# Experts' results of the last layer: weighted on leaving PSUM and added in DRAM, instead of read back and weighted at the end

## The reference, cut to what matters

```
logits = xn @ w_gate                       # xn = layernorm(h), 8 experts
top_p, top_i = top_k(softmax(logits), 2)
top_p = top_p / sum(top_p)                 # = 1/(1+e) and e/(1+e), e = exp(l2 - l1)
y_e(x) = gelu(x @ w_up[e]) @ w_down[e]     # 192 -> 768 -> 192
out = h + top_p[0] * y_i0(xn) + top_p[1] * y_i1(xn)
```

## Time and profile before

| | us |
|---|---|
| median of 3 runs (612.25 to 617.3) | 615.44 |
| profiled execution, own time | 616.41 |
| its span | 614.6 |
| PE / DVE / ACT / POOL busy | 492.7 / 325.0 / 205.1 / 143.8 |
| last mixture of experts: first gather to last result | 414.51 to 593.57 |
| from there to the end of the span | 21.0 |

### The profile page before, as it was taken

The page is one execution under the profiler, slowest core; times in us unless marked ns, Lnnn a source line. Parts: engine busy times, 40 slices in busy tenths (PEclk is TensorE's granted clock), DMA queues, the critical chain, the costliest instruction groups (busy, mean ns, idle before and its releaser), DMA issues.

```text
span 614.6 us, 12430 instructions
## 1 busy us (share of the span) xinstructions
PE 492.7 (80%) x4338; PEld 453.3 (74%) x4339; DVE 325.0 (53%) x1046; ACT 205.1 (33%) x438; POOL 143.8 (23%) x148
## 2 busy tenths in 40 slices
PE   4999999887523493699999599627999999999960
PEld 4999996466522393589999586616999999999950
DVE  1578999688999886122221576782222222222207
ACT  3620024666993164044333142150321112121110
POOL 1591000000001001334421100005345444443220
PEclk9999999899557785799999799757999999999995
DMA  8991000000004003956669300027866655667126
GB/s 311 409 335 34 1 1 1 1 3 1 0 1 181 2 2 138 241 168 180 177 202 366 127 2 0 1 103 211 237 194 194 204 171 161 185 178 204 42 63 270
DMA packets 35379, 81.41 MB, mean 132 GB/s; under 512 B 7142, under 2 KB 18242, under 8 KB 34306
## 3 DMA queue, kind: packets, MB, share of 16 engines
q1 hardware_dynamic: 29762, 69.37, 34.3%
q0 software_dynamic: 5568, 11.41, 6.5%
HBM read 70.33 MB, written 10.42 MB: 131 GB/s over the span
## 4 chain that ended last, share of the span: by engine, by line
PE 69%; DVE 17%; ACT 5%; DMA 3%; issue 3%; SPq 1%; another core or an unknown queue 1%; ACTq 0%; POOL 0%; DVEq 0%; POOLq 0%
PE ps L1102 18%; PE ps L858 14%; PE ps L1078 12%; PE ps L1086 6%; PE ps L798 2%; DVE h L1878 2%; PE ps L970 1%; PE ps L838 1%; PE ps L839 1%; PE ps L942 1%; DVE xT L1722 1%; PE ps L1069 1%; PE ps L823 1%; PE ps L943 1%; DVE arena L1586 1%
## 5 line engine op out<-in xcount | busy, mean ns | idle before, releaser
L1102 PE MATMUL ps<-arena,xn 128*128 x696 | 123.2, 328 | 3.9 <-ACT xn L748 3.1
L1102 PEld LDWEIGHTS ps<-arena,xn 128*128 128x128 f32 x696 | 111.8, 190 | 6.2 <-issue 6.0
L491 POOL DMA_INDIRECT xT<-rows,from_i x58 | 56.2, 969 | 180.5 <-DVE from_i L1736 121.8
L1078 PE MATMUL ps<-xn,arena 128*128 128x128 f32 x696 | 91.0, 282 | 5.2 <-DMA arena<-ffn_b 3.2
L858 PE MATMUL ps<-arena 128*128 128x192 f32 (+1 forms) x588 | 86.3, 339 | 8.7 <-ACT arena L530 8.7
L1078 PEld LDWEIGHTS ps<-xn,arena 128*128 128x128 f32 x696 | 87.7, 198 | 6.9 <-DMA arena<-ffn_b 5.6
L858 PEld LDWEIGHTS ps<-arena 128*128 128x128 f32 (+1 forms) x588 | 84.8, 199 | 8.9 <-ACT arena L530 8.3
L1761 DVE COPY xn<-ps 128x128 f32<-128x128 f32 x58 | 16.9, 292 | 126.7 <-PE ps L1070 94.9
L504 POOL DMA_INDIRECT made<-xT,to_i x58 | 57.2, 985 | 109.8 <-DVE xT L1773 66.6
L751 ACT ACTIVATE xn<-ps 128x384 f32<-128x384 f32 x78 | 32.6, 493 | 126.5 <-PE ps L1088 99.7
L748 ACT ACTIVATE xn<-ps,b_all 128x128 f32<-128x128 f32 x114 | 30.9, 390 | 46.8 <-PE ps L1088 35.3
(11 more groups left out here) (367 smaller groups left out, 773.9 us busy)
## 6 DMA issues: line engine op xcount, KB each, us to landing
arena<-ffn_a SPq DMA_DIRECT2D x58, 384.0 KB
arena<-ffn_b SPq DMA_DIRECT2D x116, 96.0 KB
arena<-x_blocks SPq DMA_DIRECT2D x16, 384.0 KB, 7.1
arena<-x_strips SPq DMA_DIRECT2D x3, 1536.0 KB, 11.9
arena<-ffn SPq DMA_DIRECT2D x4, 1152.0 KB
rows<-xn SPq DMA_DIRECT2D x8, 384.0 KB, 2.3
arena<-made SPq DMA_DIRECT2D x4, 768.0 KB, 6.6
arena<-tok_w SPq DMA_DIRECT2D x8, 288.0 KB, 7.3
```

The lines of the kernel that those rows point to most:

```text
L491: pool.indirect_dma_start(sx[:, k % 6], None, F["src"], bass.IndirectOffsetOnAxis(from_i[:, k:k + 1], 0)).then_inc(sem(f"sx_in{k % 6}"), 16)
L1078: pe.matmul(ps[:, up_bank(u, c // 3), 128 * (c % 3):128 * (c % 3) + 128], w_up[:, u, 128 * c:128 * c + 128], sT[:, u, 0:128], start=(c % 3 ...
L1102: mm = pe.matmul(ps[:, result_bank(k, N), 0:DIM], hT[:, u % 2, 128 * c:128 * c + 128], F["w2"][:, bass.ds(e2 + DIM * c, DIM)], start=(c == ...
```

## The change

The first expert stage and all matmuls stay. In the last stage:

- Routing makes the two weights early (DVE, before the scan): e goes into column 193 of a 200-wide row of `xw`, 1/(1+e) into column 192. ACT writes the norm into columns 0 to 191, and SP writes these rows of 800 bytes to DRAM, now after `probs` as well. The gather fetches them.
- `to_i` is the token's row. `to_use` holds, for each slot, whether its token uses it as second expert. When a tile is turned, two more DVE instructions of one column each make `p_slot`: 1/(1+e) and a factor that is 1 or e. The gather of tile k + 10 waits for `p_slot` instead of the turning.
- `result` multiplies by both numbers as it takes the result out of PSUM.
- `made1` holds one row a token. SP writes `h` into it in one DMA once `h` is final (`h_row` 14), and, near the program's start, finite numbers into the rows of the empty slots. The scatter adds to its rows (`compute_op` add), and POOL issues each only when the one before has landed.
- At the end SP copies these rows to `out` in one DMA from DRAM to DRAM. Reading back, adding on DVE and the four writes are gone.

```diff
+ROW = 200
...
-                  seg=C_SEG + E0 * 16, src=rows1, made=made1)
+                  seg=C_SEG + E0 * 16, made=made1)
...
-        pk = sb("pk", [128, 2, NTOK])
...
-        sx = xT0[:, 0:6 * DIM].rearrange("p (a b) -> p a b", a=6)
-        yo = xT0[:, 6 * DIM:9 * DIM].rearrange("p (a b) -> p a b", a=3)
-        got = [xn[:], view(0, [2 * NTOK, DIM])]
+        sx = xT0[:, 0:6 * ROW].rearrange("p (a b) -> p a b", a=6)
+        yo = xT0[:, 6 * ROW:6 * ROW + 3 * DIM].rearrange("p (a b) -> p a b", a=3)
+        xw = view(E1 * HCH * DIM, [NTOK, ROW])
+        wide_rows = made0.rearrange("r c -> (r c)")[0:TOKS * ROW].rearrange("(r c) -> r c", c=ROW)
+        to_use = sb("to_use", [128, 2, 40])
+        p_slot = sb("p_slot", [128, 2, 6])
...
+            sp.wait_ge(sem("cst_in"), 16)
+            sp.dma_start(made1[TOKS + 1:TOKS + 1 + 128 * TILES1, :].rearrange("(k p) c -> p k c", p=128),
+                         cst[:, C_ID:C_ID + DIM].unsqueeze(1).to_broadcast([128, TILES1, DIM])).then_inc(sem("sums_set"), 16)
+
             def rows_out(F):
 
+                if F["n"]:
+                    sp.wait_ge(sem("probs"), 1)
                 for i in range(4):
                     sp.wait_ge(sem("xn_act"), 4 * (1 + F["n"]) + i + 1)
-                    sp.dma_start(F["src"].rearrange("(b t) c -> b t c", t=NTOK)[:, 4 * i:4 * i + 4, :],
-                                 xn[:, 4 * i:4 * i + 4, :]).then_inc(sem(f"rows_out{F['n']}"), 16)
+                    dst, src = ((rows0, xn), (wide_rows, xw))[F["n"]]
+                    sp.dma_start(dst.rearrange("(b t) c -> b t c", t=NTOK)[:, 4 * i:4 * i + 4, :],
+                                 src[:, 4 * i:4 * i + 4, :]).then_inc(sem(f"rows_out{F['n']}"), 16)
...
-            def outputs_in(F):
-
-                n = F["n"]
+            def results_landed(F):
+
                 for u in range(3):
-                    sp.wait_ge(sem(f"y_st{n}{u}"), 16 * ((F["tiles"] + 2 - u) // 3))
-                made = F["made"][0:F["sel"] * TOKS, :].rearrange("(b r) c -> b r c", b=IMGS)
-                for i in range(4):
-                    r = slice(4 * F["sel"] * i, 4 * F["sel"] * (i + 1))
-                    sp.dma_start(got[n][:, r, :], made[:, r, :]).then_inc(sem(f"back_{i}"), 16)
+                    sp.wait_ge(sem(f"y_st{F['n']}{u}"), 16 * ((F["tiles"] + 2 - u) // 3))
...
-            outputs_in(F0)
+            results_landed(F0)
+            for i in range(4):
+                sp.dma_start(xn[:, 4 * i:4 * i + 4, :], made0[0:TOKS, :].rearrange("(b t) c -> b t c", t=NTOK)[:, 4 * i:4 * i + 4, :]
+                             ).then_inc(sem(f"back_{i}"), 16)
+            sums = made1[0:TOKS, :].rearrange("(b t) c -> b t c", t=NTOK)
+            sp.wait_ge(sem("h_row"), 14)
+            sp.dma_start(sums, h[:]).then_inc(sem("sums_set"), 16)
             rows_out(F1)
             up_weights(F1)
-            outputs_in(F1)
-            for i in range(4):
-                sp.wait_ge(sem("h_final"), i + 1)
-                sp.dma_start(out[:, 4 * i:4 * i + 4, :], h[:, 4 * i:4 * i + 4, :]).then_inc(sem("out_done"), 16)
-            sp.wait_ge(sem("out_done"), 64)
+            results_landed(F1)
+            sp.dma_start(out, sums).then_inc(sem("out_done"), 16)
+            sp.wait_ge(sem("out_done"), 16)
...
+                rows, width, turned = (rows0, DIM, "x_ps0") if n == 0 else (wide_rows, ROW, "p_slot")
+
                 def load(k):
-                    pool.indirect_dma_start(sx[:, k % 6], None, F["src"],
+                    pool.indirect_dma_start(sx[:, k % 6, 0:width], None, rows,
                                             bass.IndirectOffsetOnAxis(from_i[:, k:k + 1], 0)).then_inc(sem(f"sx_in{k % 6}"), 16)
 
...
-                        pool.wait_ge(sem(f"x_ps{n}"), k - 5)
+                        pool.wait_ge(sem(turned), k - 5)
...
                 for k in range(N):
                     pool.wait_ge(sem(f"y_out{n}"), k + 1)
+                    if n and k == 0:
+                        pool.wait_ge(sem("sums_set"), 32)
+                    if n and k:
+                        pool.wait_ge(sem(f"y_st1{(k - 1) % 3}"), 16 * ((k - 1) // 3 + 1))
                     pool.indirect_dma_start(F["made"], bass.IndirectOffsetOnAxis(to_i[:, k:k + 1], 0), yo[:, k % 3],
-                                            None).then_inc(sem(f"y_st{n}{k % 3}"), 16)
+                                            None, compute_op=(ALU.bypass, ALU.add)[n]).then_inc(sem(f"y_st{n}{k % 3}"), 16)
                     if k + 10 < N:
-                        pool.wait_ge(sem(f"x_ps{n}"), k + 5)
+                        pool.wait_ge(sem(turned), k + 5)
                         load(k + 10)
...
-                        ins = act.activation(xn[:, t, :], h[:, t, :], ACT.Identity, bias=stat[:, 480 + t:481 + t], scale=stat[:, 464 + t:465 + t])
+                        ins = act.activation((xn[:], xw)[n][:, t, 0:DIM], h[:, t, :], ACT.Identity, bias=stat[:, 480 + t:481 + t], scale=stat[:, 464 + t:465 + t])
...
-            act.activation(d16, d16, ACT.Exp).then_inc(sem("soft_exp"), 1)
+            act.activation(xw[:, :, DIM + 1], d16, ACT.Exp).then_inc(sem("soft_exp"), 1)
...
                 if n:
                     dve.tensor_tensor(d16, c16, a16, ALU.subtract).then_inc(sem("soft_in"), 1)
+                    dve.memset(xw[:, :, DIM + 2:ROW], 0.0)
+                    dve.wait_ge(sem("soft_exp"), 1)
+                    link(dve.tensor_scalar(c16, xw[:, :, DIM + 1], 1.0, None, ALU.add))
+                    dve.reciprocal(xw[:, :, DIM], c16).then_inc(sem("probs"), 1)
...
-                dve.scalar_tensor_tensor(to_i[:, 0:N], row, 0.5 * n, none, ALU.add, ALU.add).then_inc(sem("places"), 1)
-                if n:
-                    dve.wait_ge(sem("soft_exp"), 1)
-                    link(dve.tensor_scalar(c16, d16, 1.0, None, ALU.add))
-                    link(dve.reciprocal(pk[:, 0, :], c16))
-                    dve.tensor_tensor(pk[:, 1, :], d16, pk[:, 0, :], ALU.mult)
+                if n == 0:
+                    dve.tensor_tensor(to_i[:, 0:N], row, none, ALU.add).then_inc(sem("places"), 1)
+                else:
+                    dve.wait_ge(sem("places"), 3)
+                    token, second = rt[:, 1280:1280 + N], to_use[:, 1, 0:N]
+                    link(dve.tensor_copy(token, from_i[:, 0:N]))
+                    dve.tensor_tensor(to_i[:, 0:N], token, none, ALU.add).then_inc(sem("places"), 1)
+                    link(dve.scalar_tensor_tensor(second, token, -2.0, row, ALU.mult, ALU.add))
+                    link(dve.tensor_scalar(second, second, 0.5, ROUND, ALU.add, ALU.add))
+                    dve.tensor_scalar(to_use[:, 0, 0:N], second, -1.0, ROUND + 1, ALU.mult, ALU.add)
+                    link(dve.tensor_scalar(second, second, ROUND, None, ALU.subtract))
...
                     dve.tensor_copy(sT[64:128, u, 128:256], ps[0:64, 0, 128:256]).then_inc(sem(f"x_out{n}"), 1)
+                    if n:
+                        dve.tensor_copy(p_slot[:, 0, u:u + 1], sx[:, u, DIM:DIM + 1])
+                        dve.scalar_tensor_tensor(p_slot[:, 1, u:u + 1], sx[:, u, DIM + 1:DIM + 2], to_use[:, 1, bass.ds(k, 1)],
+                                                 to_use[:, 0, bass.ds(k, 1)], ALU.mult, ALU.add).then_inc(sem("p_slot"), 1)
...
                     dve.wait_ge(sem(f"b_ps{n}"), k + 1)
+                    if n:
+                        dve.wait_ge(sem("p_slot"), k + 1)
                     at_least(dve, sem(f"y_st{n}{u % 3}"), 32 * j + 16 * (u // 3))
                     if n == 0:
                         ins = dve.tensor_tensor(yo[:, u % 3], ps[:, result_bank(k, N), 0:DIM], b2_all[:, bass.ds(e, DIM)], ALU.add)
                     else:
-                        ins = dve.tensor_copy(yo[:, u % 3], ps[:, result_bank(k, N), 0:DIM])
+                        ins = dve.tensor_scalar(yo[:, u % 3], ps[:, result_bank(k, N), 0:DIM], p_slot[:, 0, u:u + 1], p_slot[:, 1, u:u + 1],
+                                                ALU.mult, ALU.mult)
                     ins.then_inc(sem(f"y_out{n}"), 1)
...
             copies(F1)
-            for i in range(4):
-                dve.wait_ge(sem(f"back_{i}"), 32)
-                for s in range(2):
-                    for t in range(4 * i, 4 * i + 4):
-                        ins = dve.scalar_tensor_tensor(h[:, t, :], got[1][:, 2 * t + s, :], pk[:, s, t:t + 1], h[:, t, :], ALU.mult, ALU.add)
-                    if s == 0:
-                        link(ins)
-                ins.then_inc(sem("h_final"), 1)
```

More of the change, by code:

```diff
@@ L1745, in route @@
                 dump, none = rt[:, 1280:1280 + N], g
-                link(dve.tensor_scalar(dump, cst[:, C_TILE:C_TILE + N], 128.0, cst[:, C_P + 1 + n:C_P + 2 + n], ALU.mult, ALU.add))
+                link(dve.tensor_scalar(dump, cst[:, C_TILE:C_TILE + N], 128.0, cst[:, C_P + 1:C_P + 2], ALU.mult, ALU.add))
                 link(dve.scalar_tensor_tensor(none, row, -0.75, dump, ALU.is_lt, ALU.mult))
```

(8 more changed lines are left out.)

## The result

| | before | changed |
|---|---|---|
| median, us (4 runs each, one chip) | 614.55 (612.25 to 617.3) | 642.44 (639.71 to 647.89) |
| profiled execution, own time / span | 616.41 / 614.6 | 641.31 / 639.5 |
| first scatter of the stage to the last | 435.50 to 593.85 | 436.30 to 628.58 |
| last scatter to the end of the span | 20.7 | 10.9 |

The changed kernel takes 1.0467 of the time before, 95% interval [1.0417, 1.0517]: 4.7% slower, above the range of 605 to 632. The end became 9.8 us shorter, and the stage before it 34 us longer.

The account below looks back on a forecast made before the run. PE's matmuls bound the middle, a chain of transfers and DVE work the end. Span 614.6 - 4.8 (end) + 0.2 (routing) = 610.0, forecast 610.8 us against the median; range 605 to 632.

Parts of the forecast that it names:

- where the forecast is thin: POOL's chain of 39 scatters in mid-stage: mean need 4.07 us against 4.17 available per tile, so no loss; called weakest step.
- S + 0.28: A tile's need in the scatter chain, issue to landing plus POOL's semaphore answer: 3.31 us quiet, 4.50 under load.
- S: Issue to landing of an adding scatter: plain 2.33 us plus 0.7 for the addition, 3.03 on quiet DMA engines.
- the prediction's mixture: Mid-stage need per tile weighted by DMA share: 0.64 x 4.50 + 0.36 x 3.31 = 4.07 us.
- the issue is paid once: Pricing an adding scatter: POOL's 0.97 us issue does not grow, only one direction of the 1.36 us trip is added.
- Rival 1: Last stage: scatters become its bound if the addition under load costs over 0.85 us; 631 us at 1.4; chance 0.32.
- The end: After the last tiles: three serial scatters 4.1 us later, copy 9.0 us, read-back and DVE work gone; 4.8 us saved.
- the prediction's sum: Final copy's time: 1.35 us besides data plus 3.8 or 7.7 us of data, giving 5.2 or 9.0 us.
- Rival 2: Final DRAM copy runs at the read-back's rate, 406 to 436 GB/s, 3.8 us less: 607 us; chance 0.17.
- The routing: Before the scan: added DVE addition and reciprocal move the scan and first gather 0.2 us later, between 0 and 0.5.
- DVE in the middle: Per tile, two one-column instructions under 0.25 us each and a 0.36 us multiplication, costed at nothing on PE and DVE.
- Work that was moved to where nothing runs: Early write of finite numbers (19 us) and write of `h` (9 us) fall in idle time, adding nothing to the path.

Follow-up runs that it names:

- the plain chain: Changed kernel with the last stage's scatters plain instead of adding, each still waiting for the landing of the one before: 605.06 us, 0.9854 of the kernel before.

## Why the prediction failed, point by point

**The middle, "where the forecast is thin": wrong, and all of the miss.** The forecast took "no loss" from a need of S + 0.28 that came out at 4.07 us, just under 4.17 (PE's mean over the stage; 4.32 in mid-stage, so the measure was even a little strict). The run shows 5.06 on average, and the last scatter at 628.58 where the prediction's own steps put it at 590.61 + 2 x 3.31 + 0.2 = 597.4, 31.2 us earlier. The span was to be 610.0 and is 639.5, 29.5 more. The difference of 1.7 is the copy and the rest of the end, which went better. Three sizes inside that step were too small. Of the 0.99 us between 4.07 and 5.06, POOL's answer makes 0.47 and the landing the other 0.52: its mean is 5.06 - 0.75 = 4.31, where the prediction's mixture of 4.22 and 3.03 gives 3.79.

- *S on quiet engines*: 3.03 taken, 3.50 measured. The addition costs 1.17, not 0.7. The prediction said "the issue is paid once"; but POOL's issue itself grows from 0.97 to 1.55 us, and that 0.58 stands in front of the trip. The trip grew from 1.36 to 1.95, by 0.59, near to the 0.7.
- *POOL's answer*: 0.28 taken from the earlier trace rows, where POOL waits for DVE. Here it waits for a landing, and answers after 0.73 to 0.77; the plain chain shows the same 0.74. With these two the need on quiet engines is 4.27 and not 3.31: before any load was counted no room was left against PE.
- *Under load*: 4.22 taken for S, from a gather beside the first weights. Measured 4.2 in the median of 434 to 560 us, and that the two agree is chance: the median lies between twelve landings of 3.5 to 3.6 and twelve of 4.8 to 6.2, with a mean of 5.4. The loaded case was 1.2 us too short, and how often it occurs cannot be had from the DMA share, which the prediction used as its weight: at a share of 0.6 plain scatters landed in 2.3 us without the wait and in 3.9 with it. And the quiet case never falls below 3.4, so that the long landings have nothing to set against them.

There was also a fault of argument. The mean of the needs was compared with the mean of the tiles, as if the one could catch up for the other. Three `yo` buffers let it do so only as long as the quiet period is well below PE's 4.32; with 4.27, and 4.3 to 4.4 with a gather between, nothing is ever caught up, and each long landing stays in the sum. The plain chain has landings under load up to 5.5 us too (median 3.9 from 434 to 560 us), and still comes out at (593.13 - 432.35) / 38 = 4.23 on average, with PE full, because its quiet period is 3.07.

**Rival 1 was the mechanism**, with 0.32 of chance. It named the point from which it decides, an addition under load of over 0.85 us. Its price of 631 used twice the taken price for the addition but kept the answer of 0.28. With 0.75 in that place its mean of 4.77 becomes 5.24, and the measured 5.06 is a little under that.

**The end: right in kind, better in size.** Reading back, DVE's 11.12 us and the last write are gone, and the three last scatters do stand in a row. The copy was taken at 9.0 us between ends of 5.2 and 9.0 and landed in 6.9. The 406 to 436 GB/s of the read-back are no limit for reads and writes together: the copy moves 3.1 MB, both ways, in 6.9 us, which is 456 GB/s with everything in it. With the 1.35 us of the prediction's sum taken off for the start, an estimate, it is some 570. The prediction's estimate by the Trainium skill's page "DMA: Bandwidth & Descriptors" (section "Latency and other measured facts"), which gives 207 to 214 GB/s each way for copies between two HBM tensors, was 8.8 us for the copy. This trace shows 6.9, and the measurement decides. Rival 2 was half right, on a kernel in which it no longer mattered.

**The routing: right, a little less than nothing.** The timeline of the changed kernel:

```profile
399.98 0.39 DVE L1709 TENSOR_TENSOR rt<-rt 128x16 f32<-128x16 f32 x1
...
400.41 0.23 ACT L802 ACTIVATE arena<-rt 128x16 f32<-128x16 f32 x1 [11.24 <-DVE rt L1709]
...
400.89 0.26 DVE L1713 RECIPROCAL arena<-rt 128x16 f32<-128x16 f32 x1
401.06 0.69 DVE L1717 TENSOR_TENSOR_SCAN rt<-cst,ps 128x256 f32<-128x256 f32 x1
```

From the subtraction to the scan it is 1.08 us, and it was 1.07: the predicted 0.2 is 0.0. In the profiled execution the whole stretch is 0.67 us later than in the one of before, from the first of these rows on, and the first gather, at 415.19, is 0.68 us later.

**DVE in the middle: right.** The two instructions on one column take 0.15 and 0.21 us, and the multiplication 0.48 where the copy took 0.36 (0.36 had been assumed). With waits out of the way PE is at 60.00 of 60 in spite of them, in seven of the eight experiments.

**Work that was moved to where nothing runs: right.** The write of finite numbers is issued at 53.9 and takes 13.4 us, so it lands long before anything asks for it; the kernel with all of this and plain scatters without waits is 9.5 us faster than the one before.

## What to carry to other kernels

Before an operation is made to wait for the landing of the one before, add up the whole period on quiet engines: issue, trip, and the waiting engine's answer to a landing, taken from a row where it waits for a DMA. If that is not well below what the bound engine needs for one step, load adds to the sum, and three buffers did not help here. Look at single landings and not at their median, which lay here between two groups. And in the profile, where an instruction waits for two semaphores, check when the one that is named first could have mattered. Ask next how many of them must stand in a row, for two at a time made the same additions free here.

## What the runs showed of the hardware

- An adding indirect scatter of 128 rows of 768 bytes takes POOL 1.59 us to issue, a plain one 0.99. It lands after 3.5 us on quiet DMA engines, a plain one after 2.33. Beside the weights' loads it took up to 7.1, and beside an eighth of them 3.9 at most.
- POOL starts its next instruction 0.73 to 0.77 us after a landing that it waits for, and 0.28 us after the end of DVE's instruction.
- One copy from DRAM to DRAM of 1.57 MB landed in 6.9 us (6.7 to 6.9 in five others). Reading back 4 x 768 KB into SBUF took 6.6 us for one piece in the kernel before.
